# A four-layer transformer on one core: the end of layer 0, its feed-forward part and layer 1's operands as one pipeline of eight chunk tails

## The reference, cut to what matters

```python
x = _layernorm(x + _L0_attn_ref(x, Wq, Wk, Wv, Wo, rms_w))   # linear attention, 16 heads of 16, RMS norm, then @ Wo
x = _layernorm(x + _L0_ffn_ref(x, weight, bias))
x = _layernorm(x + _L1_attn_ref(x, Wq, Wk, Wv, Wo, bo))      # causal softmax attention, one key and value head shared by 16 query heads
...
def _L0_ffn_ref(x, weight, bias):
    alpha = mean(abs(weight), over inputs)
    bw = where(weight >= 0, 1, -1) * alpha
    return einsum('bsi,oi->bso', x, (bw - weight) + weight) + bias
```

## Time and profile before

| | us |
|---|---|
| median of 3 runs | 1859.93 (1859.24 to 1860.58) |
| the profiled execution | 1866.14, its span 1864.3 |
| TensorE busy | 1661.6 (89% of the span) |
| TensorE weight loads | 989.7 (53%) |
| DVE busy | 1007.3 (54%) |
| ACT busy | 772.4 (41%) |
| POOL busy | 421.6 (23%) |

### The profile page before, as it was taken

One profiled execution on the slowest core, in us unless ns is written; L12 is line 12 of the kernel. 1 busy time (PEld: TensorE's weight loads), 2 busy tenths in 40 slices (PEclk: granted clock), 3 DMA queues, 4 the chain that ended last, 5 costly groups with the idle time before them and its releaser, 6 DMA issues.

```text
span 1864.3 us, 25178 instructions
## 1 busy us (share of the span) xinstructions
PE 1661.6 (89%) x9820; PEld 989.7 (53%) x9820; DVE 1007.3 (54%) x1698; ACT 772.4 (41%) x1787; POOL 421.6 (23%) x474
## 2 busy tenths in 40 slices
PE   7985688889999999869997888986999999989998
PEld 4664343333433334534565455764777777764556
DVE  4666656576777773163442864315667666741222
ACT  3420234556767776412111121115666666642110
POOL 3222301101000000140000038604344444540000
PEclk9997778899999999989998999987999999998999
DMA  4000320000000002010000030000000020000000
GB/s 155 2 2 15 85 58 2 2 1 1 2 1 2 1 2 95 1 47 0 1 0 15 0 113 0 1 0 5 7 1 7 1 78 1 1 1 1 12 12 23
DMA packets 28501, 35.07 MB, mean 19 GB/s; under 512 B 5728, under 2 KB 24864, under 8 KB 27872
## 3 DMA queue, kind: packets, MB, share of 16 engines
q1 hardware_dynamic: 28384, 33.48, 5.7%
HBM read 23.87 MB, written 2.10 MB: 14 GB/s over the span
## 4 chain that ended last, share of the span: by engine, by line
PE 67%; DVE 14%; POOL 7%; issue 7%; ACT 3%; SPq 1%; DMA 1%; POOLq 0%; DVEq 0%; ACTq 0%
PE PS L966 7%; PE PS L1244 6%; PE PS L1250 6%; PE PS L953 6%; PE PS L928 5%; PE PS L1265 5%; PE PS L2083 3%; PE PS L2072 2%; PE PS L1746 2%; PE PS L2050 2%; PE PS L1729 2%; POOL arena L2268 2%; DVE arena L1190 2%; PE PS L330 2%; PE PS L1003 2%
## 5 line engine op out<-in xcount | busy, mean ns | idle before, releaser
L1190 DVE TENSOR_REDUCE arena<-PS 128x1 f32<-128x1024 f32 (+7 forms) x320 | 329.9, 1061 | 133.1 <-PE PS L930 95.7
L1076 ACT ACTIVATE arena<-PS 128x512 f32<-128x512 f32 (+3 forms) x640 | 318.1, 533 | 165.5 <-PE PS L956 74.1
L953 PE MATMUL PS<-arena 99*128 99x512 bf16 (+3 forms) x640 | 208.7, 357 | 1.9 <-ACT arena L1076 1.4
L928 PE MATMUL PS<-arena 96*128 96x512 bf16 (+3 forms) x640 | 182.2, 363 | 24.9 <-DVE arena L1190 22.1
L190 POOL TENSOR_TENSOR rstd<-ve,mhalf 128x4 f32<-128x4 f32 x32 | 32.3, 1010 | 611.0 <-DVE ve L216 611.0
L966 PE MATMUL PS<-arena 128*32 128x512 f32 (+3 forms) x1280 | 155.0, 557 | 2.8 <-ACT arena L1082 1.7
L185 ACT ACTIVATE XT<-PS 128x1024 f32<-128x1024 f32 x32 | 32.8, 1024 | 291.3 <-PE PS L178 291.3
L953 PEld LDWEIGHTS PS<-arena 99*128 99x128 bf16 x640 | 61.0, 100 | 154.2 <-ACT arena L1076 113.7
L1244 PE MATMUL PS<-XT,arena 128*128 128x512 f32 x256 | 122.7, 602 | 5.6 <-DVE R L199 3.5
L2083 PE MATMUL PS<-arena 128*128 128x256 f32 x512 | 121.0, 379 | 2.0 <-DVE R L199 2.0
L1250 PE MATMUL PS<-XT,arena 128*128 128x512 f32 x256 | 121.2, 596 | 0.0
(11 more groups left out here) (236 smaller groups left out, 2868.4 us busy)
## 6 DMA issues: line engine op xcount, KB each, us to landing
arena<-arena SPq DMA_DIRECT2D x55, 128.0 KB, 2.4
XT<-in_L_attn_xT SPq DMA_DIRECT2D x4, 512.0 KB, 7.4
X<-in_L_attn_x SPq DMA_DIRECT2D x4, 512.0 KB, 9.2
arena<-in_L_attn_out_w SPq DMA_DIRECT2D x1, 2048.0 KB, 7.7
out<-X SPq DMA_DIRECT2D x4, 512.0 KB, 2.9
arena<-in_dmask SPq DMA_DIRECT2D x1, 1024.0 KB, 5.6
arena<-in_L_ffn_W_up SPq DMA_DIRECT2D x1, 1024.0 KB, 4.9
arena<-in_L_ffn_W_gate SPq DMA_DIRECT2D x1, 1024.0 KB, 7.0
```

Of the source, the lines that this page charges most:

```text
L928: last = pe.matmul(flat[:, o:o + w], q, a.KS[0:SROWS, CH * kc:CH * kc + w], start=True, stop=kc < c)
L953: last = pe.matmul(PS[:, b, lo:CH], a.KS[0:rows, P * j:P * (j + 1)], a.QS[0:rows, G1 * g + r, CH * c + lo:CH * (c + 1)], start=True, stop= ...
L1076: act.activation(a.PB[:, n % 3, r, lo:CH], PS[:, 4 + x % 3, lo:CH], ACT.Exp, scale=D0 ** -0.5).then_inc(a.e2, 1)
L1190: dve.tensor_reduce(dst, src, AX.X, ALU.max, negate=True).then_inc(a.m1, 1)
```

## The change

The eight tails of layer 0 (four of its attention, four of its feed-forward part) become one sequence, `EARLY = [(0, 0), (0, 1), (0, 2), (1, 0), (0, 3), (1, 1), (1, 2), (1, 3)]`, of pairs (block, chunk). Each of its steps gives its output to one of two pairs of banks and its sum to one of two buffers `R`. DVE sums step n before it normalises step n - 1. The squares and signs of the weights move into the tile loop of layer 0, the mean squares and inverse RMS are taken per chunk there, and `sumsq` goes into another bank and behind `out`. Buffers of that loop that held 16 tiles become rings of four (`RING0`) or two, so that layer 1's constants can be loaded at the start, and its value buffer lies free. The feed-forward bias is added by a matmul of one row per tile; layer 1's bias is added by POOL later, in the steps of `BIAS1_AT`. Layer 1's projections of chunks 0 and 1 are cut in two (queries; keys and values) and put between the last tails; chunks 2 and 3 follow directly. The first exponential waits for the stacks of chunks 0 and 1 alone.

```diff
-    a.VM = take([P, NT, H // 2, 2, 32])
-    a.KD = take([P, NT, E])
-    a.KTr = take([P, NT, KT, P])
-    a.QD = take([P, NT, KT, P])
+    a.VM = take([P, RING0, H // 2, 2, 32])
+    a.KD = take([P, RING0, E])
+    a.KTr = take([P, 2, KT, P])
+    a.QD = take([P, RING0, KT, P])
...
+        if n == NT:
+            l0f_sum(k, pe)
+        if 0 <= n - 3 < NT:
+            out(n - 3)
+        if n == NT + 3:
+            l0_out(k, pe, 0)
         if 0 <= n - 4 < NT:
             sumsq(n - 4)
         if 0 <= n - 3 < NT:
-            out(n - 3)
             keys_values(n - 3)
...
+def l0_out(k, pe, n):
+
+    a = k.l0
+    c = EARLY[n][1]
+    if n == 0:
+        pe.wait_ge(a.wo_s, 1)
+        pe.wait_ge(k.l0f.mean, 1)
+        pe.wait_ge(a.qT_ev, NT)
+    if n == 1:
+        pe.wait_ge(a.rs_v, NC)
+        pe.wait_ge(a.at, 2 * NT)
+    if n >= 2:
+        pe.wait_ge(k.r_done, n - 1)
...
+def l0f_out(k, pe, n):
+    a = k.l0f
+    c = EARLY[n][1]
+    if c == 0:
+        pe.wait_ge(a.bwd, 1)
+    pe.wait_ge(k.r_done, n - 1)
+    pe.wait_ge(k.xt_done, AT0[0, c] + 1)
+    for j in range(TPC):
+        t = TPC * c + j
+        F = f_tile(k, j, 2 * (n % 2))
+        pe.matmul(F, k.ones[0:1, :], a.bias[0:1, :], start=True, stop=False)
+        for kt in range(KT):
+            last = pe.matmul(F, k.XT[:, kt, P * t:P * (t + 1)], a.bw[:, kt, :], start=False, stop=kt == KT - 1)
+    last.then_inc(k.f_ready, 1)
...
+def l0f_pe(k, pe):
+    early_out(k, pe, 1)
+    for n in range(1, len(EARLY) + 1):
+        if 2 <= n + 1 < len(EARLY):
+            early_out(k, pe, n + 1)
+        early_turn(k, pe, n - 1)
+        if n == 5:
+            l1_project(k, pe, 0, 0)
+        if n == 6:
+            l1_project(k, pe, 0, 1)
+        if n == 7:
+            l1_project(k, pe, 1, 0)
+    l1_project(k, pe, 1, 1)
+    l1_project(k, pe, 2, 0)
+    l1_project(k, pe, 3, 0)
...
+    for n in range(1, len(EARLY)):
+        summed(n)
+        normed(n - 1)
+        tail_stats(k, dve, st, n, a.R[n % 2])
+        if n == 6:
+            l1_residual(k, dve, 0, 0)
+        if n == 7:
+            l1_residual(k, dve, 0, 1)
+            l1_low(k, dve, 0)
+    normed(len(EARLY) - 1)
+    l1_keys(k, dve, st, 0)
...
 def l1_sp(k, sp, I):
     a = k.l1
-    sp.wait_ge(k.xt_done, NC)
...
     stack_chunk(0)
     stack_chunk(1)
-    stack_chunk(2)
     maxima_rows(0)
+    stack_chunk(2)
+    maxima_rows(1)
     stack_chunk(3)
...
         if n == 0:
             for par in range(2):
-                act.wait_ge(a.stack[par], 16 * SPLIT_DMAS * 2)
+                act.wait_ge(a.stack[par], 16 * SPLIT_DMAS)
...
+        if n in BIAS1_AT:
+            add_bias(BIAS1_AT[n])
```

More of the change, by code:

```diff
@@ L405, in l0_pe @@
         if 0 <= n - 3 < NT:
-            out(n - 3)
             keys_values(n - 3)
[L408 to L420, removed]
-    tail_pe(k, pe, 2 * NC - 1, NC - 1)
 def l0_act(k, act, st):
@@ L468, in l0_act @@
             out(n - 3)
-    for c in range(NC):
-        tail_act(k, act, NC + c, c)
+        if n == 8:
+            l0f_magnitude(k, act)
 def l0_pool(k, pool, st):
@@ L637, in l0f_act, with l0f_sum, l0f_signs @@
     act.activation(a.abs, a.w, ACT.Abs).then_inc(a.absd, 1)
-    for c in range(NC):
-        if c == NC - 1:
-            l1_high(k, act, 0)
-        tail_act(k, act, 2 * NC + c, c)
-def l0f_pool(k, pool, st):
-    a = k.l0f
-    pool.wait_ge(a.ld, 32)
-    add_bias(k, pool, 1, a.bias, a.biased)
-    for c in range(NC):
-        tail_pool(k, pool, st, NC + c)
-def l0f_dve(k, dve, st):
+def l0f_sum(k, pe):
+    a = k.l0f
+    pe.wait_ge(a.absd, 1)
+    pe.wait_ge(k.l0.rot, NT)
+    for kt in range(KT):
+        last = pe.matmul(k.PS[:, QK0, 0:E], k.ones[:, :], a.abs[:, kt, :], start=kt == 0, stop=kt == KT - 1)
+    last.then_inc(a.sum, 1)
+def l0f_signs(k, dve, st):
     a = k.l0f
@@ L766 @@
 P1 = Plan1()
-PREP1_AT = {-7: 2, -5: 3}
+FIRST1, LAST1 = -AHEAD1, NC - 1
+HIGHS1 = [(1, 2), (4, 5), (7, 7), (9, 9)]
+VALUES1 = [3, 6, 8, 10]
+RES1 = [2, 4, 5, 6]
+BIAS1_AT = {P1.first[8 + c] + 5: c for c in range(NC)}
 def l1_alloc(k):
@@ L891, in l1_project, with l1_high @@
         for kt in range(KT):
[L892 to L893 removed]
+            last = pe.matmul(PS[:, first + (1 if c < 2 else 3), D0 * t:D0 * (t + 1)], k.XT[:, kt, P * t:P * (t + 1)],
+                             a.w[:, kt, QK1:], start=kt == 0, stop=kt == KT - 1)
     last.then_inc(a.prj, 1)
[L897 to L901 removed]
+def l1_high(k, act, c, half):
+    a, PS = k.l1, k.PS
+    act.wait_ge(a.prj, HIGHS1[c][half])
+    first = 6 if c < 2 else 4 * (c - 2)
+    part, banks = (slice(0, 2), 2) if c < 2 and half == 0 else (slice(2, 3), 1) if c < 2 else (slice(0, 3), 3)
+    act.activation(a.hb[c][:, part, :], PS[:, first:first + banks, :], ACT.Copy).then_inc(a.ev, 1)
+    if c < 2 and half == 0:
+        return
+    act.wait_ge(a.prj, VALUES1[c])
+    act.activation(a.VX[:, TPC * c:TPC * (c + 1), 0:D0],
+                   PS[:, first + (1 if c < 2 else 3), TPC * D0 * c:TPC * D0 * (c + 1)].rearrange("p (j d) -> p j d", d=D0),
+                   ACT.Copy).then_inc(a.ev, 1)
@@ new lines, in l1_middle, with l1_residual @@
+def l1_middle(k, act, c):
+    a = k.l1
+    act.wait_ge(a.res, RES1[c])
+    act.activation(a.mb[c], a.r1, ACT.Copy).then_inc(a.mid, 1)
+def l1_residual(k, dve, c, half):
+    a, PS = k.l1, k.PS
+    dve.wait_ge(a.ev, HIGHS1[c][half])
+    if c >= 1 and half == 0:
+        dve.wait_ge(a.mid, c)
+        dve.wait_ge(a.low, 2 * c - 1)
+    first = 6 if c < 2 else 4 * (c - 2)
+    part, banks = (slice(0, 2), 2) if c < 2 and half == 0 else (slice(2, 3), 1) if c < 2 else (slice(0, 3), 3)
+    dve.tensor_tensor(a.r1[:, part, :], PS[:, first:first + banks, :], a.hb[c][:, part, :], ALU.subtract).then_inc(a.res, 1)
```

358 lines of the change are left out of this document (208 added, 150 removed).

## The result

| | before | after |
|---|---|---|
| median | 1859.59 us (1859.03 to 1860.58, 4 runs) | 1839.3 us (1837.28 to 1843.32, 4 runs) |
| the profiled execution | 1866.14 us, span 1864.3 | 1839.08 us, span 1837.0 |
| first exponential of layer 1 in it | 260.09 us | 237.26 us |

The ratio is 0.9893, with a 95% interval from 0.9876 to 0.991. The change is faster by 20.3 us. The prediction said 1823.9 us, a gain of 36, with a range from 1815 to 1838: the sign is right, and the time lies 1.3 us above the range.

The account below looks back on a forecast made before the run. No engine was taken to bound the early part, but a row of hand-overs, one chunk at a time. The first exponential moving 38.3 us, less 2 for the clock, gave 36 off 1859.93: 1823.9 us, range 1815 to 1838.

Parts of the forecast that it names:

- The new start: End of layer 0's token loop: output projection still starts at 119.24 us, within 1 us.
- The bias matmuls: Feed-forward tails on TensorE: one-row bias matmuls add 1.86 us per chunk, making each output 5.58 us.
- The path of the tails otherwise: TensorE's work from output projection through the tails to chunk 0's values: 51.6 us together, ending at 170.8.
- sign of being wrong: Stated check on layer 0's tails: the forecast is wrong if they take over 6.5 us each.
- VectorE and ACT of the last tail: From the seventh tail's copy, 172.9 us, through last normalisation and keys to chunk 1's residual: ends at 180.75.
- The clock: TensorE behind pauses around the eighth turn: half rate costs 2 us, between nothing and 3.6.
- rival 1: Half-clock restart paid in full on chunk 1's rest and chunk 2's start: 3.5 us more, 1827.4 us; chance 0.23.
- From the maxima to the first exponential: Layer 1's reductions, chunk 3's split, first score and exponential: from 198.3 to 221.8 us.
- What it costs later: Layer 1: POOL's four moved bias additions cost nothing, upper bound 9.4 us; SP's second maxima row has 6 us left.
- The shift of the exponential as the measure: Whole kernel: gain equals how far layer 1's first exponential moves, since everything after it keeps its order.
- 2 gave 1839.5: Clock stays at half through chunk 3's projection: 15.6 us more than taken, 1839.5 us; chance 0.07.
- 3 gave 1838: First exponential still waits for all stacks, chunk 3's landing 14 us late: 1838 us; chance 0.03.

Follow-up runs that it names:

- e1: Changed kernel with layer 0's sum-of-squares matmul put between the two full-array projections of a later tile; 1835.17 us, 0.9874 of the kernel before.
- e3: Changed kernel with the feed-forward bias loaded into all 128 rows, divided by 128 and added by a 128-row matmul; 1828.61 us, 0.9843 of the kernel before.
- e4: Changed kernel with four unread 512-column matmuls filling each of TensorE's two pauses; median 1830.48 us, 0.9864 of the kernel before.
- e5: Changed kernel with two thirds of chunk 2's projection before the last tail's turn, the rest behind chunk 1's second half; 1835.37 us, 0.9862 of the kernel before.
- e6: Changed kernel, but the first exponential waits for all four chunks' stacks and the second maxima rows follow chunk 3's; 1850.86 us, 0.9941 of the kernel before.
- e8: The changed kernel run again without any edit, as measure for the runs beside it; 1839.92 us, 0.988 of the kernel before.
- e7: Changed kernel with sum of squares between projections, 128-row bias, and chunk 2's projection in the pauses together; 1820.55 us, 0.9783 of the kernel before.
- e2: Changed kernel with the feed-forward bias matmuls dropped, leaving the bias out of the result; 1825.57 us, 0.9823 of the kernel before.

## Why the prediction was off, step by step

The first exponential was put at 221.8 us, plus 2 for the clock, and stood at 237.26: 13.5 us late. The kernel came out 15.4 us above the forecast. What follows is that error, term by term.

- **The new start: wrong by 6.2 us**, the largest term. "TensorE starts the output projection at 119.24 us before; one adds and the other takes back about a microsecond, and I leave 119.24, within 1 us." It started at 125.40. The step looked at what was added at the loop's end and at VectorE's small steps, but not at the loop itself, in which one matmul had changed its place. A third of a microsecond in each of eleven periods is 3.7 us, and behind the last projection another 0.8; e1 took 3.7 of these 4.5 back. The Trainium skill's page TensorEngine Tiling (Array Packing), section Key Properties, says that a change of tiling mode drains TensorE: "Mode switching requires drain". The traces agree, and give it a price: 0.2 us a change in e3, 0.1 to 0.16 in e1. The other 1.7 us of the start are the clock at 13 to 19 us, which stood at 0.72 here and at 1.00 in the profiled execution of the kernel before.
- **The bias matmuls: mis-sized, 4.6 us for four chunks.** The term was 1.86 us a chunk, taken from the 128-row instruction, the upper of the two bounds. e3 shows that this is right for a 128-row matmul (5.2 us a chunk measured, 5.58 predicted). A one-row matmul costs 3.0. Its extra is the same change of shape, which no bound contained, since both were taken from rows in which like stands beside like.
- **The path of the tails otherwise: right, 1.2 us too long.** 55.0 us measured against 51.6, so 3.4 more, less than the 4.6 of the bias. (The prediction's sign of being wrong, tails of over 6.5 us each, did come: from turn to turn a tail with a feed-forward output takes 7.6 us, and 6.74 of them are that output.) Attention outputs of 3.6 to 3.7, turns of 0.9, normalisations of 1.37 to 1.38 in all eight tails, clock 1.00.
- **VectorE and ACT of the last tail: right.** From the seventh turn's copy to chunk 1's residual 7.6 us against 7.85; the terms that the prediction names for it add up to 7.73.
- **The clock: mis-sized by 3.6 us; rival 1 came true.** 190.00 to 213.15 is 23.15 us for work that was put at 17.55, so 5.6 and not 2. "I take 2, between nothing and 3.6, since these pauses are shorter than the 6.7 us that stood a microsecond ahead of that slow projection" was the wrong step: pauses of 1.86 and 2.03 us sufficed, and the value matmuls, which no row had shown slow, doubled as well. e4 and e5 show that without the pauses the fall does not come. But in e6 the same pauses cost 1.5 us, so the 2 was within what this program does, and 5.6 was the upper end of it. The Trainium skill's page TensorE: Matmul & The Clock Gate (Part 1) has the half rate as the default, from which activity releases the clock; the halved stretch behind the pauses agrees with it, and the falls under "What the runs showed", without a longer pause ahead, are not explained by it.
- **From the maxima to the first exponential: 0.7 us too short in sum.** From TensorE's first unit to the keys' end 14.7 us against 15.0; from there to the score 8.5 against 8.1, and from the score to its exponential 0.85 against 0.35. No row shows that 0.35: in the earlier trace rows the exponential waits for a DMA, and a score alone takes 0.63 us.
- **What it costs later: right, nothing.** POOL's four bias additions stand between 436.4 and 544.4 us at 2.36 us each, and from 437 to 877 us TensorE is busy 414.05 of 440 us, where the kernel before had 414.06 from 460 to 900. The 9.4 us of the upper bound did not come. SP's second row was issued 3.6 us behind the first exponential, forecast at 2.6; up to 262 us TensorE waits for no DMA.
- **The shift of the exponential as the measure: right.** It moved 22.8 us between the two profiled executions and the medians 20.3. The kernel before had been profiled 6.2 us above its median, and about 4.5 of these lay behind the exponential, if the changed kernel's 1599.7 us there is the measure for its 1604.2. The changed kernel was profiled at its median. Its exponential was compared with one that stood too late by the other 1.7, and the sum took all 6.2 off: the last 2 us of the error, by this reckoning and not by a run.

Of the rivals, 2 gave 1839.5 and 3 gave 1838, next to the measured 1839.3, and neither is what happened: chunk 3's projection took its full-rate 5.40 us, and the exponential did not wait for all stacks. A time that fits is no evidence for its mechanism; each was excluded by one row.

The range was drawn from bounds on the terms that were doubted (bias, clock, reductions) and gave the start 1 us. Its upper end held 9.4 us for a cost that was nil, and 1 for the 6.2 that came. That the time lies only 1.3 us above it is owed to this room, not to the terms.

## What to carry to other kernels

Count changes of TensorE's shape, not only columns: a one-row bias between matmuls over 128 rows cost 0.4 us for the two changes, and was cheaper over all 128 rows; a one-column matmul cost 0.44 us in all between others of another shape, and 0.12 or 0.23 beside its like. When a change moves one instruction inside a loop, measure the loop's period on the row level and multiply by its trips before anything else. Two pauses of 2 us on TensorE's path are to be priced with the half rate that can follow, here 1.5 to 5.6 us on top of their 3.9; a piece of the next step that is ready should be put there.

## What the runs showed of the hardware

- The change of array shape between one row and 128 rows takes about 0.2 us of TensorE's time each way (e3). For 32 columns and 128, e1 gives less: 0.44 us between runs of 32 columns less 0.23 or 0.12 beside its like, so 0.1 to 0.16 each way. A bias over one row costs 0.83 us a tile of 256 columns (1.69 less the product alone at 0.86), over 128 rows 0.43.
- The clock fell in a stretch with no pause in it. In e8 from 141 to 153 us it stood at 0.57 with TensorE busy 12.00 of 12 us; e4 and e6 have the same numbers, 0.57 and 12.00. The last pause ahead, 1.20 us, had ended at 138.59, and a pause of the same length in the changed kernel's first profiled execution, to 138.72, had no fall behind it. These three had 1.00 at 13 to 19 us and 0.72 at 123 to 129. The first profiled execution of the changed kernel, e1, e3, e5 and e7 had 0.72 at 13 to 19 us, and 1.00 in both later stretches. e2 had 1.00 in all three. What decides between the two patterns stays open; no run was made for it.
- e7 spread by 1.6 us over 5 runs and the changed kernel by 11.2 over 6. Whether that is chance, or the shorter and denser pipeline meeting the clock in one pattern only, was not tried.
